# A fused transformer block on one core: another order of small steps at the end of attention and between MLP groups, and a last store in two pieces

## The reference

```python
# lists: B, N, D = 2, 1024, 256; H = 1024; cond is (2, 256)
h = film(rmsnorm(x, norm1_w), cond, film1_w, film1_b)
Q, K, V = h @ q_w + q_b, h @ k_w + k_b, h @ v_w + v_b
attn = softmax(Q @ K.T * D ** -0.5)            # per sequence, one head
x = x + (attn @ V) @ proj_w + proj_b
h = film(rmsnorm(x, norm2_w), cond, film2_w, film2_b)
out = x + gelu(h @ mlp_w1 + mlp_b1) @ mlp_w2 + mlp_b2
```

## Time and profile before

| | us |
|---|---|
| median of three runs | 233.45 |
| the profiled execution, whole | 233.46 |
| its span in the trace | 231.6 |
| PE busy | 217.1 |
| DVE busy | 150.4 |
| ACT busy | 111.2 |
| POOL busy | 71.1 |

### The profile page before, as it was taken

The page is one execution under the profiler, slowest core; times in us unless marked ns, Lnnn a source line. Parts: engine busy times, 40 slices in busy tenths (PEclk is TensorE's granted clock), DMA queues, the critical chain, the costliest instruction groups (busy, mean ns, idle before and its releaser), DMA issues.

```text
span 231.6 us, 3460 instructions
## 1 busy us (share of the span) xinstructions
PE 217.1 (94%) x1260; PEld 188.4 (81%) x1260; DVE 150.4 (65%) x291; ACT 111.2 (48%) x207; POOL 71.1 (31%) x102
## 2 busy tenths in 40 slices
PE   0898999997999999999999889999999999999994
PEld 0777988885999999999999779888688868888994
DVE  0599767588899988899877683146624672436223
ACT  3168654254345455414565850494349424744440
POOL 1575852001664117444243516042203230200000
PEclk9999999999999999999999999999999999999999
DMA  5994000057867786733674404000520042002002
GB/s 169 340 410 171 3 16 29 3 187 253 232 172 252 249 273 227 238 103 141 213 247 146 164 13 171 3 0 0 189 85 0 0 167 106 3 0 91 0 3 91
DMA packets 17873, 29.86 MB, mean 129 GB/s; under 512 B 2112, under 2 KB 11840, under 8 KB 17728
## 3 DMA queue, kind: packets, MB, share of 16 engines
q1 hardware_dynamic: 15552, 21.25, 28.7%
q10 hardware_dynamic: 2304, 8.39, 9.5%
HBM read 17.58 MB, written 12.06 MB: 128 GB/s over the span
## 4 chain that ended last, share of the span: by engine, by line
PE 71%; DVE 13%; DMA 6%; issue 5%; ACT 2%; SPq 2%; ACTq 0%; DVEq 0%
PE psum L761 32%; PE psum L835 18%; PE psum L890 7%; PE psum L882 5%; PE psum L888 4%; DMA raw<-in_film_wT_dram 3%; PE psum L779 3%; DMA keys_first<-crossing 2%; DVE xn L538 2%; DVE probsT L658 2%; PE psum L773 2%; DVE hT L561 1%; DVE x_rows L727 1%; DMA crossing<-turned 1%; PE psum L753 1%
## 5 line engine op out<-in xcount | busy, mean ns | idle before, releaser
L706 DVE TENSOR_TENSOR G_all<-probs,G_all 128x512 fp32r<-128x512 f32 x32 | 22.0, 697 | 47.4 <-ACT G_all L489 47.4
L835 PEld LDWEIGHTS psum<-V_all,probsT 128*128 128x128 f32 x384 | 47.4, 188 | 5.5 <-DVE probsT L658 4.4
L835 PE MATMUL psum<-V_all,probsT 128*128 128x256 f32 x384 | 48.3, 282 | 3.3 <-DVE probsT L658 3.3
L761 PE MATMUL psum<-hT,w 128*128 128x512 f32 x192 | 49.0, 392 | 0.0
L761 PE MATMUL psum<-hT,G_all 128*128 128x512 f32 x192 | 46.5, 392 | 0.0
L489 ACT ACTIVATE probs<-psum,vcol 128x512 f32<-128x512 f32 x32 | 22.0, 689 | 47.1 <-PE psum L761 46.7
L761 PEld LDWEIGHTS psum<-hT,w 128*128 128x128 f32 x192 | 35.4, 188 | 6.7
L761 PEld LDWEIGHTS psum<-hT,G_all 128*128 128x128 f32 x192 | 35.1, 188 | 7.1
L430 ACT CAST probsT<-keys_first 128x1024 fp32r<-128x1024 f32 x16 | 16.8, 1049 | 36.9 <-DVE raw L651 17.7
L335 POOL TENSOR_TENSOR x_rows<-x_rows,add_row 128x256 f32<-128x256 f32 x16 | 11.8, 736 | 67.5 <-DVE probsT L658 67.5
L890 PE MATMUL psum<-w,G_all 128*128 128x512 f32 x84 | 30.6, 398 | 0.0
(11 more groups left out here) (72 smaller groups left out, 256.8 us busy)
## 6 DMA issues: line engine op xcount, KB each, us to landing
keys_first<-crossing SPq DMA_DIRECT2D x64, 128.0 KB, 3.0
crossing<-turned ACTq DMA_DIRECT2D x8, 512.0 KB, 3.8
crossing<-raw ACTq DMA_DIRECT2D x8, 512.0 KB, 3.6
out_dram<-x_rows SPq DMA_DIRECT2D x8, 256.0 KB, 2.6
x_rows<-in_x_dram SPq DMA_DIRECT2D x3, 512.0 KB, 9.6
rows_crossing<-raw SPq DMA_DIRECT2D x3, 512.0 KB, 2.6
raw<-rows_crossing SPq DMA_DIRECT2D x12, 128.0 KB, 2.8
raw<-in_film_wT_dram SPq DMA_DIRECT2D x2, 512.0 KB, 8.5
```

Of the source, the lines that this page charges most:

```text
L706: dve.tensor_tensor(gelu[:, m, LO, :], gelu_full[:, m % 2, :], gelu[:, m, HI, :].bitcast(F32), ALU.subtract).then_inc(gelu_ready, 1)
L761: last = pe.matmul(dst, stationary(a, k), moving(b, k), start=(n == len(tiles) * len(PASSES) - 1), stop=(n == 0))
L835: last = pe.matmul(bank(6 + t % 2, D), probsT[:, t % 2, a, k, :], V_all[:, t // KT * KT + k, s, :], start=(n == 0), stop=(n == KT * len(PA ...
```

## The change

Nothing is computed differently. These steps are moved:

- `normed_rows` and `turn_rows` of group 1 stand further ahead on DVE, `normed_rows` behind `crossed_lo(13)` and `turn_rows` behind `add_attention(12)`. POOL's `inverse_rms` for them stands one tile earlier (t = 12).
- ACT makes `crossed_hi(13)` before it starts the transfer of tile 15, not after.
- The low columns of group 0, two instructions, are split: one ahead of the last row maximum, one where both stood. POOL makes the high columns ahead of the second bias of row tile 1.
- At the borders between MLP groups (0 to 1 and 1 to 2) `normed_rows` of the group after the next stands behind the last `gelu_low` of the old group; `turn_rows` stays behind the first `gelu_low` of the new one.
- The last store, two row tiles in one transfer, becomes two transfers of one row tile.

```diff
-                for j in range(0, GT, 2):
-                    sp.wait_ge(rows_done, TILES + g * GT + j + 2)
+                for j, end in ((0, 2), (2, 3), (3, 4)) if g == GROUPS - 1 else ((0, 2), (2, 4)):
+                    sp.wait_ge(rows_done, TILES + g * GT + end)
...
+                if t == 11:
+                    high_columns(GROUPS, 0)
                 if 10 <= t < 10 + GT:
                     pool.wait_ge(xn_done, TILES + GT)
                     second_bias(t - 10)
-                if t == 11:
-                    high_columns(GROUPS, 0)
-                if t == 13:
+                if t == 12:
                     inverse_rms(GROUPS + 1)
...
             squares_after(1)
+            crossed_hi(TILES - 3)
             store_turned(TILES - 1)
-            crossed_hi(TILES - 3)
...
+                if t == TILES - 1:
+                    low_columns(GROUPS, slice(0, GW), (0,))
                 row_maximum(t)
...
                 if t == TILES - 1:
-                    low_columns(GROUPS, slice(0, GW))
+                    low_columns(GROUPS, slice(0, GW), (1,))
                 if t >= LAG:
                     turn_blocks(t)
             crossed_lo(TILES - 3)
+            normed_rows(GROUPS + 1, GT)
             add_attention(TILES - 4)
+            turn_rows(1)
...
             gelu_low(0, 2)
-            normed_rows(GROUPS + 1, GT)
-            turn_rows(1)
             crossed_lo(TILES - 1)
...
                     if m == 0 and g + 1 < GROUPS:
-                        normed_rows(g + (GROUPS + 1), g * GT + GT)
                         turn_rows(g + 1)
...
+                    if m == HT - 1 and g + 2 < GROUPS:
+                        normed_rows(g + (GROUPS + 2), g * GT + 2 * GT)
```

More of the change, by code:

```diff
@@ L248, in store_rows @@
                 b, first = divmod(g * GT, KT)
-                for j in range(0, GT, 2):
-                    sp.wait_ge(rows_done, TILES + g * GT + j + 2)
-                    sp.dma_start(out_v[:, b, first + j:first + j + 2, :],
-                                 x_rows[:, g * GT + j:g * GT + j + 2, :]).then_inc(stored, 16)
+                for j, end in ((0, 2), (2, 3), (3, 4)) if g == GROUPS - 1 else ((0, 2), (2, 4)):
+                    sp.wait_ge(rows_done, TILES + g * GT + end)
+                    sp.dma_start(out_v[:, b, first + j:first + end, :],
+                                 x_rows[:, g * GT + j:g * GT + end, :]).then_inc(stored, 16)
             cross_rows(1)
@@ L259, in _ @@
                 store_rows(g)
-            sp.wait_ge(stored, 16 * TILES // 2)
+            sp.wait_ge(stored, 16 * (TILES // 2 + 1))
         @block.gpsimd
@@ L556, in squares, with low_columns @@
                 last.then_inc(dve_sq_done, 1)
-            def low_columns(n, tokens):
-                for d in range(DT):
+            def low_columns(n, tokens, parts=range(DT)):
+                for d in parts:
                     dve.wait_ge(h_hi, n * DT + (d + 1))
```

## The result

The changed kernel takes 229.69 us (median of four runs, 229.15 to 230.44) against 233.40 for the kernel before in the same comparison (233.01 to 233.62): a ratio of 0.984, interval 0.9819 to 0.9861. The forecast was 229.3 us.

A forecast was written before the change was run, and what follows sets the result against it. PE, busy 94% of the span, was taken to bound the kernel, so time could come only from its waits: 233.46 - 2.53 (end of attention) - 1.58 (borders) - 0 (last store) = 229.35, forecast 229.3 us, own range 228.9 to 229.7.

The forecast's parts named there:

- The gaps on PE at the end of attention: PE's waits for DVE before attention(13) and attention(15), with the slower restarts: both go, 2.53 us less.
- The queue on DVE: DVE's work between crossed_lo(13) and crossed_lo(14): crossed_lo(14) ends at 133.3, 0.6 us before PE wants it.
- normed_rows did not wait for rstd: Slower rival: DVE stands at normed_rows for rstd, PE waits behind it; 234.7 us if rstd comes at 132.5; chance 0.02.
- the first gap: PE's wait before attention(13) at 129.16, ended by DVE: it goes, with a margin of 1.8 us.
- one chain: End of attention: earlier block turn and cast-first order on ACT let crossed_lo(13) run from 125.3 to 126.5.
- The borders: Two MLP group borders, where PE waits for DVE's finished rows: 0.79 us gained at each, 1.58 in all.
- the nearest row: Old-trace gelu_low begun at 139.61 during a POOL add: ended 0.54 behind that add, after 0.85 instead of 0.69 us.
- a fixed slowing of 0.16: Other reading of gelu_low beside a POOL add, not taken: the border would give 0.98 and the sum 228.97 us.
- The last store: Last transfer split in two at the program's end: no bytes move away, so 0 us gained or lost.
- The bounds: Last store: 0.38 us less if only the last 128 KB counts, 0.75 more if half-size packets cost as much each.
- The other estimate: Last store by the skill's DMA formula: halving the last transfer ends it 0.3 us sooner, taking the transfer as alone.

The follow-up runs named there:

- the run without that meeting: The changed kernel with POOL's second-bias adds of groups 2 and 3 held back until the new group's first gelu_low is done: 229.19 us, ratio 0.9819.
- the half store that found the engines idle: From the kernel with later bias adds and three end transfers, the first pair of row tiles in two, the last pair whole: 229.41 us, ratio 0.9809.

## Why the prediction was right

The time, 229.69, lies within the forecast's own range (228.9 to 229.7), but at its very edge, and with runs from 229.15 to 230.44 it is luck that it is not just outside. The three terms measured so.

- *The gaps on PE at the end of attention*: 2.53 forecast, 2.46 measured; two hidden pairs take 2.77 and 2.78 us instead of 2.74. The queue on DVE came in the order that was worked out, and shorter: the multiplications among POOL's adds took 2.11 against the 2.3 that I took, and crossed_lo(14) had a margin of 1.4 instead of 0.6. Of that 0.8, add_attention gives 0.2 (0.59 to the next start, where I took a bound of 0.8) and the multiplications 0.27 (2.03 to the next start); the rest is tenths and less in other steps. normed_rows did not wait for rstd.
- *How the first gap closes* was told in part wrong. The prediction let the cast ahead of the transfer and the earlier block turn work together, as one chain. The runs show two steps of which either closes it: undoing one costs some 0.2 us in the trace, in a later gap, undoing both costs 1.3 us. No number of the sum hung on it.
- *The borders*: 1.58 forecast, 1.68 measured. The mechanism was the one named: gelu_low(1, 0) waits for a POOL add, 0.33 longer against 0.35 worked out (159.42 + 0.54 is 159.96, not the 159.98 of the prediction, and gives 0.33 too), and the run without that meeting shortens it to 0.69. The reading that the nearest row gives a wait to the end of a POOL instruction, and not a fixed slowing of 0.16, held.
- *The last store* is the term that was mis-sized: 0 forecast, 0.25 lost. The step that failed is that transfers of equal bytes, moved without a break, end the program equally late. The packets did end almost equally late (0.04 us later), but a half transfer lands 0.56 to 0.61 us after its last packet and a whole one 0.36 to 0.41. The bounds held it (0.38 less to 0.75 more). The other estimate, 0.3 us sooner, is from the Trainium skill ("DMA: Bandwidth & Descriptors", Anatomy of one DMA), whose formula is a fit for transfers started by GpSimd; these start from SP. The traces do not agree with it here: the half store that found the engines idle landed 1.93 us after its issue, 0.1 sooner than a whole one (2.04), and the two halves at the end made the program longer.

The terms come to 0.07 less, 0.10 more and 0.25 less than forecast, together 0.22 of the 0.34 us between 229.35 and 229.69; the rest is within the runs' scatter. The profiled execution, at 229.15, lies below the forecast only because it was 0.32 us ahead before any moved step.

## What to carry to other kernels

Work moved out of a wait on a critical engine should be followed to all that it releases: here the multiplications left the border, but the adds hanging on them came along and took back a fifth of the gain (0.22 of 1.07 us at a border). Where a change bundles steps that mend the same gap, undo them one at a time and both together; alone, each seemed nearly worthless. A last store is not sure to end sooner when it is cut in two: measure from the last result to the last packet, to the landing and to the end of the span, before and after.

## What the runs showed of the hardware

- A DVE subtraction with both inputs in SBUF and a POOL add ran one after the other, each whole: gelu_low lasts 1.02 us among the adds and 0.69 without, four adds last 3.27 us beside it and 2.83 without. It waited for the end of the add that was under way and went ahead of the next one, not behind all four; it ended 0.56 us after that add, and 0.54 in the kernel before. The block turn and the adds from PSUM ran beside POOL at their usual length.
- Four multiplications of 128x256 on DVE took 2.11 us beside two POOL adds, and 1.14 without.
- A store of 128 KB in packets of 1 KB landed 0.56 to 0.61 us after its last packet, one of 256 KB in packets of 2 KB 0.36 to 0.41, with or without another right ahead.
- SP's issue of one of these stores lasts 0.33 us, and 0.43 to 0.45 when it directly follows another issue.
